# Narrow products beside wide ones, attention in the gather's banks, and new orders for two halves

## The reference

```
q, k, v = xn @ qkv_w + qkv_b                   # 16 heads of 16 channels
q, k    = q / |q|, k / |k|                     # per token and head
attn    = (q @ (k^T v)) @ proj_w + proj_b      # k^T v: 16 x 16 for each head, over the batch's 1024 tokens
ffn     = relu(xn @ W1 + b1) @ W2 + b2         # 256 -> 1024 -> 256
out     = x + attn + ffn
```

## Time and profile before

| | |
|---|---|
| Median of three runs | 551.58 us (551.14 to 551.66) |
| Span of the profiled execution | 549.6 us; its device time is not on the page, the runs lie about 2.0 us above the span |
| PE busy | 544.7 us, 99%, 2824 matmuls |
| Weight loads | 465.4 us, 85% |
| DVE busy | 437.9 us, 80% |
| ACT busy | 313.2 us, 57% |
| POOL busy | 189.1 us, 34% |
| Granted clock of PE | 1.00 over the span |

### The profile page before, as it was taken

The page is one execution under the profiler, slowest core; times in us unless marked ns, Lnnn a source line. Parts: engine busy times, 40 slices in busy tenths (PEclk is TensorE's granted clock), DMA queues, the critical chain, the costliest instruction groups (busy, mean ns, idle before and its releaser), DMA issues.

```text
span 549.6 us, 9448 instructions
## 1 busy us (share of the span) xinstructions
PE 544.7 (99%) x2824; PEld 465.4 (85%) x2824; DVE 437.9 (80%) x856; ACT 313.2 (57%) x594; POOL 189.1 (34%) x196
## 2 busy tenths in 40 slices
PE   9999999999999999999999999999999999999997
PEld 7888788888888888888888888888888888888896
DVE  6977889688796987969788697987879778794846
ACT  4785734665537665474754656647565574734521
POOL 4242587320272312623235232543126340280010
PEclk9999999999999999999999999999999999999999
DMA  8422134352233424134251342524324242141723
GB/s 273 165 77 48 38 84 92 84 107 73 63 69 85 100 72 101 33 84 100 72 103 31 87 99 70 95 39 110 75 71 87 43 100 48 36 79 21 149 62 78
DMA packets 141415, 45.37 MB, mean 83 GB/s; under 512 B 133330, under 2 KB 136402, under 8 KB 141396
## 3 DMA queue, kind: packets, MB, share of 16 engines
q1 hardware_dynamic: 139280, 44.61, 35.1%
q10 hardware_dynamic: 2116, 0.53, 0.5%
HBM read 20.98 MB, written 8.39 MB: 53 GB/s over the span
## 4 chain that ended last, share of the span: by engine, by line
PE 91%; SPq 4%; ACT 3%; DVE 1%; issue 1%; DMA 0%; ACTq 0%
PE o_bank L1453 11%; PE o_bank L1454 11%; PE o_bank L1455 11%; PE w_bank L1453 10%; PE w_bank L1454 10%; PE w_bank L1455 10%; PE v_bank L1453 6%; PE v_bank L1455 6%; PE v_bank L1454 6%; SPq L372 4%; PE kv_bank L1629 2%; PE g_bank L1629 2%; PE kv_bank L1634 1%; PE g_bank L1634 1%; PE kv_bank L1647 1%; PE w_bank L1685 1%
## 5 line engine op out<-in xcount | busy, mean ns | idle before, releaser
L719 ACT ACTIVATE h_hi<-w_bank 128x512 fp32r<-128x512 f32 x128 | 75.6, 596 | 50.1 <-PE w_bank L1455 50.1
L1453 PE MATMUL w_bank<-xT_hi,w_hi 128*128 128x512 f32 x254 | 100.2, 394 | 0.2 <-DVE h_lo L1159 0.2
L1454 PE MATMUL w_bank<-xT_lo,w_hi 128*128 128x512 f32 x254 | 99.5, 392 | 0.0
L1455 PE MATMUL w_bank<-xT_hi,w_lo 128*128 128x512 f32 x254 | 98.9, 390 | 0.0
L1159 DVE SCALAR_TENSOR_TENSOR h_lo<-w_bank,h_hi 128x512 fp32r<-128x512 f32 x128 | 85.9, 680 | 15.2 <-ACT h_hi L719 13.5
L438 POOL TENSOR_TENSOR xn_lo<-xn,xn_hi 128x256 fp32r<-128x256 f32 x56 | 41.9, 748 | 151.2 <-ACT xn_hi L598 147.0
L1453 PE MATMUL o_bank<-h_hi,w_hi 128*128 128x512 f32 x240 | 93.8, 391 | 0.0
L1454 PE MATMUL o_bank<-h_lo,w_hi 128*128 128x512 f32 x240 | 93.8, 391 | 0.0
L1455 PE MATMUL o_bank<-h_hi,w_lo 128*128 128x512 f32 x240 | 93.4, 389 | 0.0
L486 POOL TENSOR_TENSOR y_sb<-y_sb,y_rows 128x256 f32<-128x256 f32 x56 | 62.9, 1127 | 9.4 <-DVE y_rows L1203 5.3
L1453 PEld LDWEIGHTS w_bank<-xT_hi,w_hi 128*128 128x128 f32 x254 | 47.9, 188 | 10.3 <-DVE h_lo L1159 1.9
(11 more groups left out here) (246 smaller groups left out, 1267.8 us busy)
## 6 DMA issues: line engine op xcount, KB each, us to landing
y_rows<-blocks SPq DMA_DIRECT2D x256, 32.0 KB, 1.9
x_sb<-x SPq DMA_DIRECT2D x15, 512.0 KB, 3.3
y_sb<-x SPq DMA_DIRECT2D x60, 128.0 KB, 3.1
out<-y_sb SPq DMA_DIRECT2D x58, 128.0 KB, 2.5
xT_raw<-blocks SPq DMA_DIRECT2D x224, 32.0 KB, 1.9
y_sb<-w SPq DMA_DIRECT2D x4, 256.0 KB, 5.4
x_sb<-x SPq DMA_DIRECT2D x2, 256.0 KB, 3.1
w_raw<-w SPq DMA_DIRECT2D x2, 256.0 KB, 7.1
```

What stands on the lines that cost most here:

```text
L719: nc.scalar.activation(h_hi[:, j % RING, :], w_bank[j % 2][:], ACT.Relu).then_inc(h_done, 1)
L1453: nc.tensor.matmul(to, left[0], right[0], start=first, stop=False, skip_group_check=shared)
L1454: nc.tensor.matmul(to, left[0], right[1], start=False, stop=False, skip_group_check=shared)
L1455: return nc.tensor.matmul(to, left[1], right[0], start=False, stop=last, skip_group_check=shared)
```

## The change

- `product` and everything built on it become generators that pause after each matmul. `alone` runs one to its end. `beside(narrow, wide)` issues three matmuls of the wide step, three of the narrow one, three wide, and then the rest of the narrow; with `each` = 2 it is six narrow at a time.
- In the loop's halves the 256-column steps stand beside an `ffn_up` or `ffn_down`: `qk_begin` with `ffn_up(4)` now ahead of the gather, and so on. The gather alternates one matmul of 512 columns with one of 256.
- `attend` of the even half writes g_bank and kv_bank instead of v_bank, and the wait for `yT_added` moves from `qk_begin` (and `query_key`) to the gather of the even half.
- ACT's and DVE's lists of both halves are new. SP's and POOL's lists are the same. Batch 0 and the last batch keep their orders.

```diff
@@ -852,54 +852,54 @@
 
             def even_half(b, s):
                 h_high(s, 2)
+                x_forms_high(s + 1)
                 k_high(s, 0)
+                h_high(s, 3)
+                qk_seed(s + 1, 0)
+                h_high(s, 4)
+                h_high(s, 5)
+                ln_root(s + 2)
+                qk_pair_out(s + 1, 1, 0, 0)
+                qT_high(s, 0)
+                normalise(s + 2, 0)
+                h_high(s, 6)
+                qk_pair_out(s + 1, 1, 0, 1)
+                qk_seed(s + 1, 1)
+                h_high(s, 7)
+                xn_high(s + 2, 0)
+                h_high(s + 1, 0)
+                qk_pair_out(s + 1, 1, 1, 0)
+                qk_pair_out(s + 1, 1, 1, 1)
+                h_high(s + 1, 1)
+                yT_out(b, 0, 0)
+                qk_root(s + 1)
+                xT_high(s + 2, 0)
+                yT_out(b, 0, 1)
+
+            def odd_half(b, s):
                 x_forms_high(s + 1)
+                h_high(s, 2)
                 h_high(s, 3)
+                k_high(s, 1)
                 h_high(s, 4)
                 qk_seed(s + 1, 0)
+                g_high(b)
+                h_high(s, 5)
                 ln_root(s + 2)
-                h_high(s, 5)
-                normalise(s + 2, 0)
-                qk_pair_out(s + 1, 1, 0, 0)
-                xn_high(s + 2, 0)
-                qk_pair_out(s + 1, 1, 0, 1)
-                qk_seed(s + 1, 1)
-                qT_high(s, 0)
-                h_high(s, 6)
-                h_high(s, 7)
-                qk_pair_out(s + 1, 1, 1, 0)
-                qk_pair_out(s + 1, 1, 1, 1)
-                h_high(s + 1, 0)
-                qk_root(s + 1)
-                yT_out(b, 0, 0)
-                yT_out(b, 0, 1)
-                h_high(s + 1, 1)
-                xT_high(s + 2, 0)
-
-            def odd_half(b, s):
-                h_high(s, 2)
-                k_high(s, 1)
-                x_forms_high(s + 1)
-                h_high(s, 3)
-                g_high(b)
-                ln_root(s + 2)
-                h_high(s, 4)
-                qk_seed(s + 1, 0)
-                h_high(s, 5)
-                normalise(s + 2, 1)
                 qk_pair_out(s + 1, 0, 0, 0)
                 h_high(s, 6)
+                normalise(s + 2, 1)
+                qk_pair_out(s + 1, 0, 0, 1)
+                h_high(s, 7)
+                qk_seed(s + 1, 1)
                 xn_high(s + 2, 1)
-                qk_pair_out(s + 1, 0, 0, 1)
-                qk_seed(s + 1, 1)
-                h_high(s, 7)
+                h_high(s + 1, 0)
                 m_high(b)
+                qT_high(s, 1)
                 qk_pair_out(s + 1, 0, 1, 0)
                 qk_pair_out(s + 1, 0, 1, 1)
-                h_high(s + 1, 0)
+                h_high(s + 1, 1)
                 qk_root(s + 1)
-                qT_high(s, 1)
-                h_high(s + 1, 1)
                 xT_high(s + 2, 1)
 
             def last_even_half(b, s):
@@ -1189,7 +1189,7 @@
...
-                nc.vector.tensor_tensor(to, in_pairs((last_banks if last else v_bank)[k][:]), to, ALU.add).then_inc(yT_added, 1)
+                nc.vector.tensor_tensor(to, in_pairs((last_banks if last else g_banks)[k][:]), to, ALU.add).then_inc(yT_added, 1)
@@ -1309,66 +1309,66 @@
                 divide(1, 0, k_done)
 
             def even_half(b, s):
+                h_low(s, 2)
+                xT_low(s + 1, 1)
                 divide(0, 0, q_done)
-                h_low(s, 2)
+                x_forms_low(s + 1)
                 k_low(s, 0)
                 transpose_q(s, 0)
-                xT_low(s + 1, 1)
                 h_low(s, 3)
-                x_forms_low(s + 1)
+                h_low(s, 4)
+                qk_seed(s + 1, 0)
                 variance(s + 2, b + 1, 0)
-                h_low(s, 4)
+                h_low(s, 5)
+                qk_sum(s + 1, 0)
+                sum_pair_squares(s + 1, 0, 0)
                 spread(s + 2)
-                qk_seed(s + 1, 0)
-                qk_sum(s + 1, 0)
                 transpose_x(s + 2)
-                h_low(s, 5)
-                sum_pair_squares(s + 1, 0, 0)
+                h_low(s, 6)
+                sum_pair_squares(s + 1, 0, 1)
                 qk_seed(s + 1, 1)
-                sum_pair_squares(s + 1, 0, 1)
-                h_low(s, 6)
                 h_low(s, 7)
+                h_low(s + 1, 0)
                 qk_sum(s + 1, 1)
                 qT_low(s, 0)
                 sum_pair_squares(s + 1, 1, 0)
                 sum_pair_squares(s + 1, 1, 1)
                 bound(s + 1)
+                h_low(s + 1, 1)
                 norms(s + 1)
-                h_low(s + 1, 0)
                 divide(1, 1, k_done)
-                h_low(s + 1, 1)
 
             def odd_half(b, s):
+                xT_low(s + 1, 0)
+                h_low(s, 2)
+                x_forms_low(s + 1)
                 divide(0, 1, q_done)
-                h_low(s, 2)
-                transpose_q(s, 1)
                 k_low(s, 1)
-                xT_low(s + 1, 0)
                 h_low(s, 3)
-                x_forms_low(s + 1)
                 variance(s + 2, b + 1, 1)
+                qk_seed(s + 1, 0)
+                g_low(b)
+                h_low(s, 4)
                 spread(s + 2)
-                g_low(b)
-                qk_seed(s + 1, 0)
-                h_low(s, 4)
                 h_low(s, 5)
                 qk_sum(s + 1, 0)
+                transpose_q(s, 1)
                 mask_kv(b)
+                h_low(s, 6)
                 transpose_x(s + 2)
                 sum_pair_squares(s + 1, 0, 0)
-                h_low(s, 6)
+                h_low(s, 7)
+                qk_seed(s + 1, 1)
+                h_low(s + 1, 0)
                 sum_pair_squares(s + 1, 0, 1)
-                qk_seed(s + 1, 1)
-                h_low(s, 7)
                 qk_sum(s + 1, 1)
                 m_low(b)
+                qT_low(s, 1)
                 sum_pair_squares(s + 1, 1, 0)
                 sum_pair_squares(s + 1, 1, 1)
                 bound(s + 1)
-                h_low(s + 1, 0)
+                h_low(s + 1, 1)
                 norms(s + 1)
-                qT_low(s, 1)
-                h_low(s + 1, 1)
                 divide(1, 0, k_done)
 
             def last_even_half(b, s):
@@ -1451,8 +1451,28 @@
             def product(to, left, right, first=True, last=True, shared=False):
 
                 nc.tensor.matmul(to, left[0], right[0], start=first, stop=False, skip_group_check=shared)
+                yield
                 nc.tensor.matmul(to, left[0], right[1], start=False, stop=False, skip_group_check=shared)
+                yield
                 return nc.tensor.matmul(to, left[1], right[0], start=False, stop=last, skip_group_check=shared)
+
+            def alone(*steps):
+                for step in steps:
+                    for _ in step:
+                        pass
+
+            def beside(narrow, wide, each=1):
+
+                for n, _ in enumerate(wide):
+                    if n % 3 == 2:
+                        for _ in range(3 * each):
+                            next(narrow, None)
+                alone(narrow)
+
...
@@ -1503,23 +1521,23 @@
...
             def qk_begin(s, u, n, batch):
 
-                if n == 0 and u == 1:
-                    wait(pe, yT_added, KC * batch)
                 if n == 0:
                     wait(pe, xT_hi_done, KC * (s + 1))
                     wait(pe, xT_lo_done, KC * (s + 1))
                 wait(pe, qk_copied, TILES * s + 2 * n - 1)
-                product(qk_11, (xT_hi[:, u, 0, tile(n)], xT_lo[:, u, 0, tile(n)]),
-                        (wqk_hi[:, 0, 0:C], wqk_lo[:, 0, 0:C]), True, False, shared=True)
+                yield from product(qk_11, (xT_hi[:, u, 0, tile(n)], xT_lo[:, u, 0, tile(n)]),
+                                   (wqk_hi[:, 0, 0:C], wqk_lo[:, 0, 0:C]), True, False, shared=True)
+                yield
                 wait(pe, xf_lo_done, s - FORMS_FROM + 1)
-                qk_form(qk_22, X11_X01, w_form(W_FIVE), n).then_inc(qk_begun, 1)
+                begun = yield from qk_form(qk_22, X11_X01, w_form(W_FIVE), n)
+                begun.then_inc(qk_begun, 1)
 
             def qk_form(to, x_form, weights, n):
...
@@ -1624,14 +1653,13 @@
                 wait(pe, k_lo_done, s + 1)
                 if u == 0:
                     wait(pe, m_lo_done, b)
+                    wait(pe, yT_added, KC * b)
                 for t in range(TILES):
                     for k in range(KC):
-                        nc.tensor.matmul(g_banks[k][:], xn_hi[:, u, t, k * P:(k + 1) * P],
-                                         k_parts[:, t].rearrange("p w n -> p (w n)"),
+                        rows = slice(k * P, (k + 1) * P)
+                        nc.tensor.matmul(g_banks[k][:], xn_hi[:, u, t, rows], k_parts[:, t].rearrange("p w n -> p (w n)"),
                                          start=u == 0 and t == 0, stop=False, skip_group_check=True)
```

(100 more changed lines are left out.)

216 lines of the change are left out of this document (75 added, 141 removed).

## The result

The changed kernel takes 644.44 us (median of four runs, 643.78 to 646.56), the one before 551.37 us beside it (551.14 to 551.66): 1.169 times as long (95% interval 1.1675 to 1.171). Forecast were 632 us and a range of 595 to 658. The profiled execution has a span of 643.2 us, 93.6 more than before.

A forecast was written before the change was run, and what follows sets the result against it. PE, busy 99%, was taken as the bound. The new lists' loop through SP's moves adds 13.3 us an iteration, 80 us in six, other terms about 0: span 549.6 + 80 = 630, plus 2.0, so 632 us; range 595 to 658.

The forecast's parts named there:

- The loop (part 3): New ACT and DVE orders delay SP's q and x moves: 79.9 us an iteration instead of 66.6; chance 0.70.
- that 10.1: Even half, from ACT's first work on landed x through DVE's operations to q transposed: 10.1 us.
- The upper price in the prediction: All of DVE's long operations stretched as divide is, and the clock: +3.5 us an iteration, 653 us.
- Part 1, alternation: PE's alternated wide and narrow products: nothing taken, between -1.0 and +0.2 us an iteration.
- the bounds: Spacing inside PE's undisturbed triples: narrow products at 0.113 the upper bound, wide ones at 0.233 the lower.
- Part 2: Even-half attention in the gather's banks, yT_added awaited at the gather: cost nothing, over 7 us of cover.
- The waits that were named: ACT for x 12 times, several us each, for q 6 times some 4 us; PE's at ffn_down and ffn_up.
- A: PE stays the bound and alternation does what it can: 546 us, or 552 with nothing won; chance 0.10.
- B: Only one chain reaches PE, say even-half qT_high in time; odd-half end's wait remains: 577 us; chance 0.06.
- C: PE's waits also lower its clock, on the loop in the odd half: up to 3 us an iteration, 650; chance 0.12.
- D: Waits exceed the loop since a queue counted free is not (POOL's add_rows before q move): over 655 us; chance 0.02.

The follow-up runs named there:

- e4: The kernel before with one line moved: in DVE's odd-half list transpose_q stands behind qk_sum; 587.25 us (1.0652).
- e2: The changed kernel with one line moved: in ACT's even-half list qT_high stands behind h_high(7) instead of ahead of normalise; 624.82 us (1.1344).
- e9: The changed kernel with SP's q moves of the loop and last batch issuing 8 instead of 16 DMAs; 602.03 us (1.0898).
- e7: The changed kernel with POOL's add_rows of the loop adding 8 of 256 columns; 630.58 us (1.1435).
- e12: The kernel before with only the gather changed: its 512- and 256-column matmuls alternate one by one; 551.95 us (1.0014).
- e6: The kernel before, its lists kept, with the gather alternating and query-key products by threes beside ffn_up or ffn_down; 602.12 us (1.0924).
- e3: The changed kernel with both lines moved, those of e1 and e2; 602.23 us (1.0912).
- e10: e3 with yT_out(b, 0, 1) ahead of xT_high, h_high(2) ahead of x_forms_high, and divide of q first in both halves; 586.56 us (1.0644).
- e5: The changed kernel with the old ACT and DVE lists, except DVE's even-half qk_seed(1) behind h_low(6); 640.1 us (1.1596).
- e11: The kernel before with even-half attention in g_bank and kv_bank, yT_added awaited at the gather, no qk_copied wait; 551.15 us (0.9998).
- e8: The changed kernel with matmuls of zeros: 15 ahead of the even half's ffn_down(0), 20 ahead of ffn_up(s + 1, 1, 0); 648.05 us (1.174).
- e1: The changed kernel with one line moved: in DVE's odd-half list transpose_q stands behind k_low instead of qk_sum; 621.74 us (1.1285).

## Why the prediction was right, and where it was not

**The loop (part 3), the main term.** Right in place and nearly in size: 81.7 us an iteration for 79.9. e4 shows the odd half's late `transpose_q` as a cause by itself (+36 us in the kernel before, undone in the changed one -22.7), e2 the even half's early `qT_high` (-19.6), e9 SP's serial issue as what they delay (-42.4). Segment by segment, from one `xT_high` to the next: odd 41.3 us measured for 41.8; even 40.5 for 38.1. From x in place to q transposed in the even half were forecast 10.1 us and measured 12.4; all other legs hold within a microsecond. Inside the odd half's leg POOL's `x_forms` was counted at 4.1 us and took 2.9.

**The term that was mis-sized** is that 10.1. It counted `xT_low`, `x_forms_low` and `k_low` at their undisturbed 1.2 us and stretched `divide` alone. The row that warned of it was used: `divide` at a mean of 1.66 against 1.2 for the same size. After the change POOL's `add_rows` runs beside all four, because SP issues the loads that it waits for right behind the move of x (the load of `y_sb` lands at 255.24 and POOL begins at 255.39), and e7 gives 13.9 us back by taking the additions away. Six iterations of 81.7 for 79.9 us are 10.8 of the 12.4 us between 644.4 and 632; the rest lies outside the loop. The upper price in the prediction (+3.5 an iteration, for all of DVE's long operations and the clock) covered it. On this pair the Trainium skill ("SBUF — State Buffer", Who interferes with whom) says that a DVE instruction with two inputs in SBUF contends with a GpSimd one that reads SBUF, and one with a single input doesn't. The rows agree: the subtractions and the multiplication are stretched, the `STREAM_TRANSPOSE` beside the same additions keeps its 1.29 us. That section of the Trainium skill calls the shared ports an exclusive lock. The rows show both sides stretched: operations of 1.22 us grew by 0.53, and POOL's additions, 0.75 us beside the transposes, took up to 1.72 beside them:

```profile
260.06 1.72 POOL L486 TENSOR_TENSOR y_sb<-y_sb,y_rows 128x256 f32<-128x256 f32 x1
...
263.53 0.75 POOL L486 TENSOR_TENSOR y_sb<-y_sb,y_rows 128x256 f32<-128x256 f32 x1
```

**Part 1, alternation: "I take nothing" came out right in this sum, but by luck.** The loop through SP was the longer one, which the term's reasons don't mention. The spacing of issue is what it said. PE after, undisturbed:

```profile
218.46 0.28 PE L1453 MATMUL v_bank<-wqk_hi,xT_hi 128*128 128x256 f32 x1
...
218.81 0.40 PE L1453 MATMUL w_bank<-xT_hi,w_hi 128*128 128x512 f32 x1
...
219.50 0.28 PE L1453 MATMUL v_bank<-wqk_forms_hi,xf_hi 128*128 128x256 f32 x1
```

Three wide 0.69 us and three narrow 0.35 lie within the bounds, and e12 puts the finest mixing at +0.75 us for the kernel. What the prediction didn't ask is when a spread step's result comes, and it put nothing for that. e6 shows +51 us for alternation with in-order lists that were made for unmixed steps. In the changed kernel the loop through SP is long enough to account for the time without it; whether it is what e3 and e10 uncover isn't shown. How the 35 us that remain in e10 divide between the spreading, `qk_begin` ahead of the gather (which waits 1.2 us five times), the moved x that still comes late and the lists stays open: e5 and e6 show that orders and lists don't add up, so no single edit isolates it.

**Part 2** cost nothing, as said (e11).

**The waits that were named.** 12 of ACT for x, and PE's at the even half's `ffn_down(0)` and at `ffn_up(s + 1, 1, 0)`, are there at the forecast 4 to 5 us; but ACT stands several us for x at the end of the odd halves alone. ACT waited 13 times for q, not 6: q's landing is late in the odd half as well, off PE's path. At the odd half's `ffn_down(0)` and (2) PE stands 1.5 us an iteration and not 5, and PE's share is 90 and not 85%: products at half clock fill the time, and e8, which lifts the clock in the even half, has the first of these waits at 3.2 us instead of 0.9. Mean clock 0.949 means that about a tenth of the span runs at 0.50, and half of that, 33 us, is the rise of PE's busy time (34.2).

**Rivals.** A (PE stays the bound) fell with the first view. B (one chain only, with `qT_high` in time) is what e2 makes of the kernel: the wait that B left is there (23.9 us in six, as before e2), but it takes 624.8 us for B's 577, since 19.5 us of waits at the odd half's `ffn_down(0)` come up; e1, the other way round, takes 621.7. C (the clock on the loop): the clock did fall, over longer stretches than C had (some 10 us an iteration for 6), but in the even half, where PE has slack, and not in the odd half, where C put it; e8 restores more than half of it and wins nothing, so there it filled slack. D (POOL ahead of the q move): the chain names POOL's additions ahead of the even half's q move, yet the move needs the first half's four alone (over by 260.1), and starts 0.13 us after the transposes end (262.78 + 1.29 = 264.07, against 264.20). POOL acted through DVE's durations and not through its queue.

## What to carry to other kernels

Where engines work through fixed lists, follow each moved step to the queue that it feeds before its own duration is counted: a DMA issue of 10.3 us that is off the path has only as much slack as the step that triggers it leaves. Interleaving two steps delays the end of the one that stood first, so the lists behind it have to be checked against the new times of arrival; put ahead of each other only items in the order in which their data arrive. Price a loop with the durations that its operations have beside their new neighbours, not with those from quiet stretches.

## What the hardware showed

- Around the end of PE's waits of 4 to 5 us the granted clock was 0.50 (1.2 GHz) for 3.4 to 6.8 us, and wide products started 0.427 us apart instead of 0.227; over the kernel this took 5% of the mean clock, and filling those waits, which gave 3 of the 5 back, won nothing (e8).
- Two-input DVE operations of 128x1024 took 1.75 us beside POOL's additions and 1.22 without them (e7); of 128x512, 1.19 and 0.64. POOL's additions of 128x256 took 0.75 us beside DVE's transposes and up to 1.72 beside those operations.
- SP issued the 16 small DMAs of a move in 10.3 us in most moves of every kernel here, 0.64 us each; a few, most of them in the first 155 us, took up to 11.8.
